# Splitting GpSimd's conversions of count tiles, converting two of them ahead of the node loop, and moving the last low parts ahead of conversions

## What is computed

```python
x = _layernorm(x + relu(h @ W1 + b1) @ W2 + b2)                  # end of layer L0, tile by tile
# L1, twice:  h = relu(h @ W_self + (segment_sum(h[src], dst) / max(deg_in, 1)) @ W_neigh + b)
x = _layernorm(x + h / max(norm(h), 1e-12))
# L2: agg = segment_sum((x * rsqrt(deg_out))[src], dst);  h = agg @ W  (batch norm follows later)
```

## Time and profile before

| | |
|---|---|
| three runs | 2273.95, 2283.13 and 2283.44 us, median 2283.13 |
| the profiled execution | 2265.46 us, its span 2263.6 us |
| busy over the span | PE 61%, DVE 49%, ACT 42%, POOL 45% |
| TensorE clock granted | 0.783 of full speed, mean |
| node loop | 948 to 1016 us of the span |
| three passes with the counts | 1016 to 1384 us of the span |

### The profile page before, as it was taken

One profiled execution on the slowest core, in us unless ns is written; L12 is line 12 of the kernel. 1 busy time (PEld: TensorE's weight loads), 2 busy tenths in 40 slices (PEclk: granted clock), 3 DMA queues, 4 the chain that ended last, 5 costly groups with the idle time before them and its releaser, 6 DMA issues. The chain is left out here.

```text
span 2263.6 us, 31513 instructions
## 1 busy us (share of the span) xinstructions
PE 1374.9 (61%) x7941; PEld 1111.6 (49%) x7941; DVE 1103.9 (49%) x2948; ACT 945.8 (42%) x1997; POOL 1019.1 (45%) x990
## 2 busy tenths in 40 slices
PE   4322247767677799699979897513545444445566
PEld 2100014445555577588968895213445334434554
DVE  5411149864354477454965413503444434435666
ACT  0101037774455487165516554421434333333424
POOL 5577710006666600023445341575555565665234
PEclk9555569888888799899989997756767767767777
DMA  4222212225555552155544360365667666667521
GB/s 144 63 67 67 67 55 89 102 97 184 161 190 187 166 176 64 45 190 191 188 141 158 123 233 29 113 168 144 193 181 197 171 200 189 178 189 195 153 62 42
DMA packets 214478, 314.19 MB, mean 139 GB/s; under 512 B 31638, under 2 KB 160149, under 8 KB 214224
## 3 DMA queue, kind: packets, MB, share of 16 engines
q1 hardware_dynamic: 111130, 153.97, 21.6%
q0 software_dynamic: 33488, 81.02, 12.6%
q10 hardware_dynamic: 69734, 77.65, 10.8%
HBM read 223.87 MB, written 88.67 MB: 138 GB/s over the span
## 5 line engine op out<-in xcount | busy, mean ns | idle before, releaser
L440 POOL DMA_INDIRECT fr_ring<-table,src_i x392 | 380.3, 970 | 399.4 <-SPq L708 269.4
L1781 POOL DMA_INDIRECT e_kv<-kv_table,e_idx x392 | 391.1, 998 | 260.2 <-DVE e_msg L1867 141.3
L736 PE MATMUL fe_ps<-fe_space 128*128 128x400 bf16 x591 | 179.5, 432 | 240.4 <-issue 158.5
L736 PEld LDWEIGHTS fe_ps<-fe_space 128*128 128x128 bf16 x591 | 86.5, 146 | 333.4 <-issue 307.7
L828 DVE TENSOR_SCALAR fe_space<-fe_space,fr_key 128x400 bf16<-128x400 f16 x591 | 160.1, 324 | 171.2 <-remote 82.7
L1816 PE MATMUL e_p<-e_msg,e_mask 128*128 128x144 f32 x784 | 140.0, 343 | 124.5 <-issue 86.8
L1795 PE MATMUL e_q<-e_qs,e_mask 128*128 128x136 f32 x784 | 153.3, 369 | 93.4 <-issue 53.4
L1049 POOL CAST ly_af<-ly_au 128x3200 fp32r<-128x3200 uint16 x47 | 134.3, 2868 | 167.4 <-DVE ly_part L1418 74.0
L782 ACT ACTIVATE fe_space<-fe_ps 128x800 uint16<-128x800 f32 x100 | 83.5, 835 | 293.0 <-PE fe_ps L736 192.7
L1816 PEld LDWEIGHTS e_p<-e_msg,e_mask 128*128 128x128 f32 x784 | 129.8, 238 | 138.4 <-issue 109.6
L1795 PEld LDWEIGHTS e_q<-e_qs,e_mask 128*128 128x128 f32 x784 | 140.4, 266 | 100.5 <-issue 96.8
(11 more groups left out here) (394 smaller groups left out, 3105.8 us busy)
## 6 DMA issues: line engine op xcount, KB each, us to landing
ly_au<-edge_counts SPq DMA_DIRECT2D x88, 800.0 KB, 4.5
sums_att<-e_row ACTq DMA_DIRECT2D x56, 532.0 KB
q_starts<-fe_space SPq DMA_DIRECT2D x56, 476.0 KB
e_qs<-q_starts SPq DMA_DIRECT2D x56, 476.0 KB
fe_edge<-in_edgesT ACTq DMA_DIRECT2D x98, 256.0 KB
edge_counts<-fe_space ACTq DMA_DIRECT2D x25, 800.0 KB
e_drow<-dst_short SPq DMA_DIRECT2D x56, 224.0 KB
fr_ring<-table,src_i POOLq DMA_INDIRECT x392
```

The lines of the kernel that those rows point to most:

```text
L440: pool.indirect_dma_start(f.ring[:, n % RB, t, 0:D], None, tab[0][:, :], bass.IndirectOffsetOnAxis(ap=src_i[:, at:at + 1].bitcast(U32), ax ...
L736: nc.tensor.matmul(ps[:, bass.ds(at, NW)], left(n), right(n % IS), start=False, stop=True, skip_group_check=True).then_inc(c["item"], 1)
L1781: pool.indirect_dma_start(kv[s][:, t, :], None, kv_table[:, :], bass.IndirectOffsetOnAxis(ap=idx[s][:, t:t + 1].bitcast(U32), axis=0)).the ...
```

## The change

1. Count tiles 0 and 1 are loaded first of all, ahead of the 13 loads for `pick`, and both are converted by POOL before its `low0` loop. Before, tile 0 was converted by POOL after `low0(21)` and tile 1 by ACT after the node loop.
2. POOL converts each tile in five instructions of 640 columns in place of one of 3200.
3. PE's wait for the last residual of the node loop moves from ahead of group 0 to the first `product`, the first that writes to the same PSUM bank.
4. `low_after` sends the last low parts of a pass one or more conversions earlier: `h_low` 11 and 12 come before the conversion of group 15, `x_low` 23 to 25 before that of group 28.

```diff
@@
-                    return m % NT % 2 == 1 and (m // NT != 1 or m % NT % 6 == 1)
+                    return m != 1 and m % NT % 2 == 1 and (m // NT != 1 or m % NT % 6 == 1)
@@
+                def at_load(m):
+
+                    return m if m < 2 else NC + m
+
                 def landed_counts(eng, m):
-                    q = NC + m
+                    q = at_load(m)
@@
-                    return min(g + 4, NG + AF - 1) if g < NG else min(g + 5, 2 * NG + AF - 1)
+                    return min(g + 4, NG + 1) if g < NG else min(g + 5, 2 * NG + 1)
@@
-                            if AS <= q < NC + AS:
-                                c.ready(sp, "picked", q - AS)
-                            elif q >= NC + AS:
-                                made(sp, q - AS - NC)
-                            if q < NC:
+                            before_it = q - AS
+                            if 2 <= before_it < NC + 2:
+                                c.ready(sp, "picked", before_it - 2)
+                            elif before_it >= 0:
+                                made(sp, before_it if before_it < 2 else before_it - NC)
+                            if 2 <= q < NC + 2:
@@
-                                    pool.tensor_copy(counts_of(m), au[(NC + m) % AS][:, :, :]).then_inc(c["by_pool"], 1)
+                                    for a in range(0, NT, NS):
+                                        part_in = pool.tensor_copy(counts_of(m)[:, a:a + NS, :], au[at_load(m) % AS][:, a:a + NS, :])
+                                    part_in.then_inc(c["by_pool"], 1)
@@
+                        convert(0)
                         for n in range(NT):
                             low0(n)
-                            if n == NT - 4:
-                                convert(0)
@@
                         in_steps(0, NT, [(0, turn0), (1, up), (2, down)])
                         pe.wait_ge(copied, 1)
-                        c0.ready(pe, "res", NT - 1)
@@
-                            if g >= 2:
+                            if g < 2:
+                                c0.ready(pe, "res", NT - 1)
+                            else:
@@
                         def pick(k):
-                            dve.wait_ge(landed[k % AS], (k // AS + 1) * 16)
+                            q = k + 2
+                            dve.wait_ge(landed[q % AS], (q // AS + 1) * 16)
```

More of the change, by code:

```diff
@@ L1026, in _ @@
                         for q in range(NC + 3 * NT):
-                            if AS <= q < NC + AS:
-                                c.ready(sp, "picked", q - AS)
-                            elif q >= NC + AS:
-                                made(sp, q - AS - NC)
-                            if q < NC:
+                            before_it = q - AS
[4 more added lines that the diff above has]
+                            if 2 <= q < NC + 2:
                                 sp.wait_ge(ids, 4)
-                                tile = sp.value_load(tile_no[0:1, q:q + 1], min_val=0, max_val=NT - 1)
+                                tile = sp.value_load(tile_no[0:1, q - 2:q - 1], min_val=0, max_val=NT - 1)
                                 sp.dma_start(au[q % AS][:, :, :], cnt[bass.ds(tile, 1), :, :].rearrange("o p (a e) -> p (o a) e", e=P)).then_inc(landed[q % AS], 16)
                             else:
-                                sp.dma_start(au[q % AS][:, :, :], cnt[(q - NC) % NT].rearrange("p (a e) -> p a e", e=P)).then_inc(landed[q % AS], 16)
+                                sp.dma_start(au[q % AS][:, :, :], cnt[q if q < 2 else (q - NC) % NT].rearrange("p (a e) -> p a e", e=P)).then_inc(landed[q % AS], 16)
                     @block.gpsimd
@@ L1228, in convert @@
                                         counts_free(act, m)
-                                        nc.scalar.activation(counts_of(m), au[(NC + m) % AS][:, :, :], ACT.Copy).then_inc(c["by_act"], 1)
+                                        nc.scalar.activation(counts_of(m), au[at_load(m) % AS][:, :, :], ACT.Copy).then_inc(c["by_act"], 1)
                         def corr_high(g):
@@ L1356, in pick @@
                         def pick(k):
-                            dve.wait_ge(landed[k % AS], (k // AS + 1) * 16)
+                            q = k + 2
+                            dve.wait_ge(landed[q % AS], (q // AS + 1) * 16)
                             e = dve.value_load(column[0:1, k:k + 1], min_val=0, max_val=P - 1)
-                            dve.tensor_copy(picked_f[:, :, k:k + 1], au[k % AS][:, :, bass.ds(e, 1)]).then_inc(c["picked"], 1)
+                            dve.tensor_copy(picked_f[:, :, k:k + 1], au[q % AS][:, :, bass.ds(e, 1)]).then_inc(c["picked"], 1)
                         def residual0(n):
```

## The result

| | before | after | ratio (95% interval) |
|---|---|---|---|
| median, beside each other | 2283.28 us (4 runs, 2273.95 to 2284.80) | 2253.12 us (4 runs, 2242.34 to 2261.66) | 0.9878 (0.9839 to 0.9917) |
| the same two kernels again | 2278.68 us (11 runs) | 2248.35 us (6 runs) | 0.9865 (0.9837 to 0.9892) |

The change makes the kernel faster, by 1.2 to 1.4%. Forecast were 2258.0 us and 1.1%; both medians lie in the range of 2242 to 2271 us.

The account below looks back on a forecast made before the run. The prediction took PE's gaps and the slow clock behind them as the bound in the block. Gains of 5.9 + 5.2 + 8.2 + 5.8 = 25.1 us off 2283.1 gave 2258.0 us, range 2242 to 2271.

Parts of the forecast that it names:

- The parts' price: POOL's conversion of a tile in five parts: taken as 3.4 us in place of 2.87, nearly all of it hidden.
- Step 1: Group 0, early tiles: PE's gap ahead of it shrinks from 8.02 to about 2.35 us; gain 5.9 us.
- Step 2: Low parts at the second pass's start: the 5.06 us gap on h_low goes; gain 5.2 us (4.4 to 6.8).
- The clock comes back earlier too: 0.8 us: Start of the second pass, behind the h_low gap: PE's faster clock returns sooner, 0.8 us, ends 0 and 2.4.
- Step 3: PE's wait for chosen 16: DVE's chain shortens by 8.1 us, the 7.76 us wait goes; gain 8.2 us (6 to 9.5).
- Step 4: Rest of the second pass: gaps of 1.00 and 2.24 us go, 4.16 shrinks; gain 5.8 us (3.5 to 7.5).
- Rival 1: Second pass: held by ACT, so DVE's saved time returns as waits on ACT; gain 15 us, 2268; chance 0.15.
- Rival 2: POOL becomes the bound as a tile's parts cost more than its idle time per group; slower, 2294; chance 0.03.
- Rival 3: POOL keeps the port across its parts, so DVE waits for whole runs of them; gain 8 us, 2275; chance 0.08.
- the three boundaries: POOL's four conversions in a row before: DVE got in as one ended, though POOL had another ready; 9.9 us lost.
- Rival 4: Node loop: the early part alone fails, as late pick or POOL's parts delay it by 5.9 us; 2264; chance 0.06.

Follow-up runs that it names:

- Run 1: The kernel before with only POOL's conversions cut into five parts: block 420.8 us, time 2273.60 us.
- run 3: The kernel before with only the early loads and conversions of tiles 0 and 1 and PE's moved wait, conversions whole: block 433.5 us, time 2288.47 us.
- run 4: The changed kernel with whole conversions, early tiles and moved low parts kept: block 420.6 us, time 2274.12 us.
- run 9: The changed kernel once more, unchanged: block 409.9 us, median 2248.35 us, ratio 0.9865 to the kernel before.
- run 6: The changed kernel with 25 parts of 128 columns a tile in place of five: block 466.5 us.
- Run 2: The kernel before with only low_after changed, conversions whole: block 427.3 us, time 2273.51 us.
- run 8: As run 7, with tile 28 also given to ACT and h_low 10 ahead of group 14's conversion: block 403.0 us, time 1747.95 us, ratio 0.978.
- run 5: The changed kernel with two parts a tile (1664 and 1536 columns) in place of five: block 412.1 us.
- run 7: The changed kernel with tile 2 converted by POOL between its low parts and tile 3 by ACT behind its last relu: block 407.1 us.

## Why the prediction was right

- **Its reading of the bound held.** In the block PE's idle time fell from 40.8 to 16.9 us and its busy time, at a higher clock, from 395.9 to 393.1: that is the 26.7 us. No gain elsewhere is shown. 26.7 us were gained in the first pair of traces, 28.3 in the second (438.2 and 409.9), 25.1 were forecast. The medians fell by 30.2 and 30.3 us, 2 to 3.5 more than the blocks; with runs of one kernel 11 to 19 us apart, that is no finding.
- **The parts' price** was taken as 3.4 us for a tile from a pair of subtractions; five parts in a row take 3.38 us by POOL's timeline. Run 1 shows the price as forecast where it isn't hidden, and in after it is seen at the 3.70 us gap.
- **Step 1** gave 5.5 of 5.9 us. The gap was 2.41 for 2.35, and the clock fell some 1.3 us behind it. Runs 3 and 4, with whole conversions, have 1.88 there and gain 7.6: the slow clock didn't follow.
- **Step 2** gave 4.6 of 5.2. The two gaps became one as forecast. That it is 3.70 us long is in part chance: in run 9 PE did some of the work ahead of it at a slow clock (0.57 from 1130 to 1134 us), and the gap was 2.13 us and ended at the same place. The term that failed is "The clock comes back earlier too: 0.8 us": the clock fell only some 1 us after PE had resumed (0.96 from 1140 to 1141, 0.50 from 1142 on), PE stayed at the lower level (1.2 GHz, matmuls 0.21 us apart) until 1147.5, and the some fifty aggregates from there took 8.45 us where they took 8.29 before. Taking 0 there, the sum's lower end, is right to 0.2 us.
- **Step 3** gave 8.5 of 8.2. DVE's four instructions waited 1.3 us in all where 1.8 was taken (0.66, 0.39 and 1.27 less 0.23, 0.17 and 0.61; the 0.23 is the shortest of this instruction, in run 6), and the `chosen` wait went.
- **Step 4** was undersized, 7.5 for 5.8. My sum had the gaps of 1.00 and 2.24 us, 1.4 of the 4.16 and 1.3 for the clock. Two gaps of before's timeline that I left out as small, 0.39 us at 1213.12 and 0.95 at 1274.97, went as well: 0.39 + 1.00 + 2.24 + 0.95 + 1.54 = 6.1. The clock gave 1.4 on balance: some 2.2 came back with the gaps, and 0.8 was lost at the start, where 16 of group 17's aggregates ran 0.21 us apart in after and 7 in before. The profile names nothing for the gap of 1.00 us ("issue" in the earlier trace rows), which the prediction puts down to ACT; ACT's conversion L1229 there ends at 1238.45 us, 0.10 ahead of PE's matmul, so the reading stands. Run 2 shows that the 1.54 us ahead of L1164 come with `low_after` alone. So the term that was mis-sized is the small gaps, put at nothing: 1.3 us of the 1.7 that this step gave beyond its forecast.
- **Rival 1** (into ACT) had been given 0.15. ACT is still what PE's 2.77 us gap ends at, but at the size forecast; the gaps at ACT's work went with DVE's. **Rival 2** didn't happen: parts are 0.67 us; it does at twenty-five parts, seven of its 13 gaps in the second pass (up to 4.09 us), where POOL converts up to four tiles in a row and the 4.58 us of idle time that the prediction leans on, from the first pass, don't stand ahead of each. **Rival 3** didn't: no instruction of L1441 or L1447 in after takes over 0.82 us, one part and its own time. Run 6 has such waits at parts of 0.24 us, so the bound that I drew from the three boundaries held for 0.67 us parts, but isn't a rule. **Rival 4** didn't: the last `down` is at 68.0 for 67.9.
- What the traces of before couldn't have told: the stages ahead of the block. Two traces of before enter it at 947.0 and 947.2 us, the eight of this length with an edit between 949.0 and 959.4 (two of after: both 951.8). In before and after the last gather starts at the same time (799.5 and 799.0 us), and the loop with L758 then ends 4.8 us later. The second pair of traces has the same (800.1 and 799.6 us, then 4.5 later). No run tells why, and whether the executions without a trace have it too isn't known.

## What to carry to other kernels

When GpSimd and VectorE share work in one stage, look in VectorE's timeline for tiny instructions with long durations, and see at which GpSimd instruction's end they end: the length of one GpSimd instruction is what such a hit costs, so cut it into a few parts, of about the length that VectorE can bear to lose. Here two, five and twenty-five parts gave blocks of 412, 410 and 467 us. With whole conversions and the change's other edits it was 421, and before 437. So of what the parts give the first cut brings nearly all, and cutting further to five shows nothing. At twenty-five the 0.13 us more for each part turn it round, and VectorE is at times kept waiting across many parts. And read the gain of one edit beside the others: the head start of run 3 was for the most part eaten by the very collisions that the parts remove.

## What the runs showed of the hardware that I had not expected

- A VectorE instruction beside GpSimd's conversions got in at the latest at the end of the running one, of 2.86 us in before and of 0.73 us in after. But in rows of conversions started every 0.24 us two VectorE instructions took 4.47 and 10.93 us, across some 18 and 45 of them, and four more 1.31 to 3.96 us; others in such rows took 0.17 to 0.35. What decides isn't known.
- A further GpSimd conversion in a row costs 0.13 us: 2.86 us for one of 3200 columns, 3.38 for five of 640; and (6.04 - 2.86)/24 = 0.13 again for 25 of 128.
- Behind a gap of PE the clock doesn't always fall: after 2.61 us ahead of L1164 in run 2 the 16 matmuls took 2.05 us, after 2.62 us in after 3.44 us, and after 2.62 us in run 8 3.57 us. A sum that prices "gap above so much, so much lost to the clock" is off by up to 1.5 us there. The node loop, in which PE has no gap of over 0.4 us but one of 1.8 at its very start, took 2.7 us more in runs 5, 6 and 8 than in run 7.
- The same kernel before took 1786.92 us beside runs 5 to 8 and 2280 beside all others, while the blocks agree as far as they can be compared (two parts, 412.1 us, in the first; five parts, 410.0, in the second). No trace of before itself was taken at 1786.92. The difference is in the gathers: before its block, POOL's L440 in run 5 took 389.5 us with 134.1 us of idle time, in after 379.2 with 400.5, of which 270.0 on SP's L708 and in run 5 11.5. So the gain has to be read in microseconds of the block, and not as a share of the time.
